# Two more of ten probability copies on ScalarE, placed between its exponentials, and high parts of the attention output on GpSimd

## The reference

```
x = x + attn(layernorm(x))          # 16 heads of 16; q and k layer-normed per head; causal softmax
x = x + ffn(layernorm(x))
  ffn:  h = h + attention(rmsnorm(h))      # 16 heads of 64, latent kv of rank 32, rope on 32, causal softmax
        h = h + moe(rmsnorm(h))            # one shared expert, 8 routed experts of 128, the best 2 chosen
attention:  att = softmax(mask(q k^T));  y = att v;  y @ Wo
```

## Time and profile before

| | us |
|---|---|
| median of 3 runs (3696.23 to 3699.96) | 3697.05 |
| the profiled execution's own time | 3699.16 |
| span of its profile, first to last instruction | 3697.5 |

### The profile page before, as it was taken

How to read it: one execution, slowest core, us unless ns; L and a number is a source line. 1 busy time by engine, 2 the same in 40 slices (tenths; PEclk the granted TensorE clock), 3 DMA queues, 4 the chain that set the end, 5 groups by cost and what they waited for, 6 DMA issues and landing times.

```text
span 3697.5 us, 82731 instructions
## 1 busy us (share of the span) xinstructions
PE 3354.6 (91%) x31744; PEld 2632.8 (71%) x31744; DVE 2763.8 (75%) x5950; ACT 2406.8 (65%) x6426; POOL 1085.9 (29%) x778
## 2 busy tenths in 40 slices
PE   2599999999999999999999999999999999999998
PEld 2477677776767777677776767777677776767776
DVE  3676877878777776877778777777877778777775
ACT  1666667666676766667666676766667666676764
POOL 0424222242412424222242412424222242412420
PEclk9799999999999999999999999999999999999999
DMA  3000000000000000000000000000000000000000
GB/s 80 1 7 1 13 2 7 7 7 7 1 13 2 7 7 1 13 1 7 7 7 7 1 13 2 7 7 1 13 2 7 7 7 7 2 13 2 7 2 7
DMA packets 33766, 28.95 MB, mean 8 GB/s; under 512 B 8864, under 2 KB 33312, under 8 KB 33376
## 3 DMA queue, kind: packets, MB, share of 16 engines
q1 hardware_dynamic: 33376, 23.68, 2.2%
HBM read 15.28 MB, written 8.39 MB: 6 GB/s over the span
## 4 chain that ended last, share of the span: by engine, by line
PE 71%; ACT 14%; DVE 10%; issue 3%; POOL 1%; SPq 1%; DMA 0%; ACTq 0%; POOLq 0%; DVEq 0%
PE bank L670 14%; PE scores L782 11%; PE bank L681 8%; ACT prob L953 6%; PE scores L657 5%; PE bank L806 5%; PE scores L733 4%; PE scores L658 4%; PE scores L756 3%; PE bank L617 3%; PE bank L641 3%; PE scores L659 3%; DVE negmax L1192 2%; ACT qkt L898 2%; PE scores L653 1%
## 5 line engine op out<-in xcount | busy, mean ns | idle before, releaser
L953 ACT ACTIVATE prob<-scores,negmax 128x128 f32<-128x128 f32 (+3 forms) x2048 | 1057.8, 535 | 186.3 <-DVE negmax L1192 180.6
L1192 DVE TENSOR_REDUCE negmax<-scores 128x1 f32<-128x128 f32 (+3 forms) x2048 | 872.6, 481 | 56.9 <-PE scores L659 42.4
L670 PE MATMUL bank<-ident,prob 128*128 128x128 f32 x5120 | 725.6, 279 | 50.6 <-DVE probt L1200 43.6
L1200 DVE COPY probt<-bank 128x512 f32<-128x512 f32 x896 | 596.1, 683 | 171.0 <-PE bank L670 165.3
L670 PEld LDWEIGHTS bank<-ident,prob 128*128 128x128 f32 x5120 | 544.1, 141 | 163.6 <-issue 66.6
L659 PE MATMUL scores<-mask,ident 128*128 128x128 bf16 x2048 | 438.1, 225 | 0.0
L953 ACT ACTIVATION_READ_ACCUMULATOR prob<-scores,negmax 128x1 f32 x2048 | 436.1, 213 | 0.0
L657 PE MATMUL scores<-khh,qt 128*128 128x256 f32 (+2 forms) x1024 | 416.3, 407 | 13.3 <-POOL kll L545 13.3
L486 POOL TENSOR_TENSOR otl<-onm,oth 128x512 fp32r<-128x512 f32 x96 | 122.6, 1277 | 888.8 <-ACT oth L898 888.8
L497 POOL TENSOR_TENSOR rq<-ssq,expo 128x32 f32<-128x32 f32 x64 | 359.9, 5632 | 39.6 <-DVE ssq L1163 39.6
L481 POOL COPY rexp<-rsum 128x512 f32<-128x512 f32 x128 | 78.0, 610 | 981.8 <-DVE rsum L1204 981.8
(11 more groups left out here) (187 smaller groups left out, 6654.6 us busy)
## 6 DMA issues: line engine op xcount, KB each, us to landing
x_in<-in_x_rows SPq DMA_DIRECT2D x16, 512.0 KB, 3.8
out_rows<-x SPq DMA_DIRECT2D x16, 512.0 KB, 2.9
r_gu<-in_wg SPq DMA_DIRECT2D x2, 512.0 KB, 5.0
r_gu<-in_wu SPq DMA_DIRECT2D x2, 512.0 KB, 5.7
r_d<-in_wd SPq DMA_DIRECT2D x1, 1024.0 KB, 7.1
r_wqt<-in_wq_nope_t SPq DMA_DIRECT2D x1, 512.0 KB, 6.7
r_wqr<-in_wq SPq DMA_DIRECT2D x2, 256.0 KB, 8.3
r_wob<-in_wo SPq DMA_DIRECT2D x1, 512.0 KB, 5.3
```

The source lines that it names most:

```text
L670: ins = nc.tensor.transpose(bank[4 + n % 2][:, q * P:(q + 1) * P], prob[:, u % 2, q, i * P:(i + 1) * P], ident[:, :])
L953: nc.scalar.activation(prob[:, u % 2, q, 0:n], bank[q][:, 0:n], ACT.Exp, bias=negmax[:, a, u, q:q + 1], accum_out=sums[:, a, u, q:q + 1]). ...
L1192: nc.vector.tensor_reduce(negmax[:, a, u, M * part:M * part + M], scores[:, M * part:M * part + M, 0:n], axis=AX.X, op=ALU.max, negate=Tru ...
L1200: nc.vector.tensor_copy(probt[:, u % 2, i], bank[4 + n % 2][:, :]).then_inc(probt_dve.sem, 1)
```

## The change

ScalarE's blocks become 0, 2, 4, 7 and 9 of ten, and each is copied behind a given exponential of the next unit: `COPY_AFTER` maps a block to the `part` behind which it stands. VectorE keeps blocks 1, 3, 5, 6 and 8. So on ScalarE the copy of block 0 stands between the second and third exponential of t1 (ahead of the output copy), that of block 2 between the third and fourth exponential of t2, that of block 4 between the third and fourth of t3, and those of blocks 7 and 9 behind all four of the next t0. For all groups but the last of an attention, GpSimd makes the high part from `onm` itself, just ahead of its subtraction, and ScalarE does not. The high part of the last group stays on ScalarE.

```
-ACT_COPIES = tuple(n in (2, 5, 8) for n in range(NT * (NT + 1) // 2))
+COPY_AFTER = {0: 1, 2: 2, 4: 2, 7: 3, 9: 3}
+
+def copy_after(n):
+    return COPY_AFTER.get(n % (NT * (NT + 1) // 2))

 def acts(n):
-    return ACT_COPIES[n % len(ACT_COPIES)]
+    return copy_after(n) is not None
...
 # GpSimd, spread_sums
+                pool.wait_ge(onm_ready.sem, onm_ready.at(b, a * NG + g + 1))
+                nc.gpsimd.tensor_copy(oth[:, g], onm[:, :]).then_inc(oth_ready.sem, 1)
                 pool.wait_ge(oth_ready.sem, oth_ready.at(b, a * NG + g + 1))
...
 # ScalarE, attend
-                if u < UNITS and here:
-                    for part in range(NM // 2):
-                        exps(b, a, u, part)
-                if u % NT == 1 and u > NT:
-                    copy_out(b, a, u // NT - 1)
-                if 0 < u <= UNITS:
-                    mine = [i for i in range(tile_of(u - 1) + 1) if acts(first_block(u - 1) + i)]
-                if u < UNITS and here:
-                    for part in range(NM // 2, NM):
-                        exps(b, a, u, part)
-                for i in mine:
-                    copy_block(b, a, u - 1, i)
-                if u % NT == 2 and u > NT:
-                    split_out(b, a, u // NT - 1)
+                if u > 0:
+                    mine = [i for i in range(tile_of(u - 1) + 1) if acts(first_block(u - 1) + i)]
+                for part in range(NM):
+                    if u < UNITS and here:
+                        exps(b, a, u, part)
+                    for i in mine:
+                        if copy_after(first_block(u - 1) + i) == part:
+                            copy_block(b, a, u - 1, i)
+                    if part == NM // 2 - 1 and u % NT == 1 and u > NT:
+                        copy_out(b, a, u // NT - 1)
```

## The result

The changed kernel takes 3747.55 us (median of 4 runs, 3746.21 to 3748.88); the kernel before, timed beside it, 3697.97 (4 runs, 3696.23 to 3699.96). The ratio of the changed to the kernel before is 1.0134, 95% interval 1.0116 to 1.0151: slower by 49.6 us, where 46.9 were forecast. The profiled span grew from 3697.5 to 3744.8 us, by 47.3.

The account below looks back on a forecast made before the run. TensorE's own work bounds the second attention, a loop through three engines the first. Per sequence 1.60 us (first attention) + 1.33 (second), times 16 = 46.9, on 3697.05 gives 3744 us; own range 3725 to 3762.

Parts of the forecast that it names:

- K: New chain: block 4's transposes, ScalarE copy, t3's fourth exponential, next t0's fourth score; at least 2.04 us.
- Steady groups of the second attention, 0.12: Next t0's fourth score comes 2.04 us behind the transposes of block 4 instead of 1.92: 0.12 us per group.
- First group of the second attention, 0.56: Copy of block 0 delays t1's third exponential, 0.44 us, plus 0.12 from block 4's copy: 0.56 us.
- Last group of the second attention, 0.53: Transposes of blocks 6, 7 come 2.04 us behind those of 4, 5, instead of 1.51: 0.53 us.
- Steady groups of the first attention, 0.23: t3's fourth exponential starts at 1517.29 instead of 1517.06, behind block 4's copy: 0.23 us late per group, nothing given back.
- step (4): First attention, steady group: t0's fourth score 0.23 us late; VectorE's block 5 copy precedes t0's maxima, first exponential some 0.3 later.
- step (3): First attention, steady group: without the high-part copy ScalarE idles for block 4; t3's fourth exponential 0.23 us late, gain eaten.
- First group of the first attention, 0.91: Copies of blocks 0, 2 and 4 bring t0's fourth score at 1714.74 instead of 1713.83: 0.91 us; no removed high-part copy helps.
- A: Rival: relieved VectorE pulls the first attention's loop along, t1's maxima 0.4 us earlier; faster, 3678 us; chance 11%.
- B: Rival: the busier of VectorE and ScalarE paces the first attention, falling by 0.03; no change, 3695 us; chance 7%.
- C: Rival: each ScalarE copy ahead of an exponential takes 0.61 us instead of 0.48; slower still, 3773 us; chance 11%.
- D: Rival: only the first groups pay, for copy of block 0, 0.48 and 0.44 us; 3712 us; chance 9%.

Follow-up runs that it names:

- the four-block kernel: Kernel before, with high parts on GpSimd and ScalarE copying blocks 2, 5, 9 behind the exponentials, 7 between t0's third and fourth: 3686.86 us, ratio 0.9966.
- the three-block one: Kernel before (ScalarE copies blocks 2, 5, 8 behind the exponentials), with only the high parts moved to GpSimd: 3686.36 us, ratio 0.9966.

## Why the prediction was right

- **What bounds each attention.** Held. The second attention's steady group is still full of TensorE's work (15.20 of 15.20), the first's is a loop through three engines, and taking 256 copies from VectorE brought it nothing.
- **K = 0.69 + 0.48 + 0.87 = 2.04.** Measured 0.69 + 0.50 + 0.82 = 2.01. The last term was read where three exponentials of 512 stand ahead of the fourth without a copy between; behind a copy it is 0.82. The run with block 4 one exponential earlier shows K as a chain: it grew by one exponential.
- **Steady groups of the second attention, 0.12.** Measured 0.09, as K is 2.01. I had written it as a wait that the score's row would show; the row shows none (1604.59 in the first group), and only its distance from the transposes, 2.01 in place of 1.92, tells of it.
- **First group of the second attention, 0.56.** Measured 0.53; the 0.44 for the copy of block 0 goes with the experiment that removed it (48.93 to 48.48, 0.45). The step that I estimated at 0.61 is 0.63 (1596.15 to 1596.78).
- **Last group of the second attention, 0.53.** Measured 0.40. K took 2.01, which adds 0.50 to the 1.51 of before, and TensorE reaches the output projection with all of it. Inside the projection 0.11 is taken back: from its first weight load to the first add it is 4.72 us before (1632.59 to 1637.31) and 4.61 in the changed kernel (1654.56 to 1659.17), at a granted clock of 1.00 in both. Why is open.
- **Steady groups of the first attention, 0.23.** Measured 0.24, by the steps: t3's fourth score waits 0.94 (0.9), block 5 waits 0.29 (0.3), t0's fourth score 0.48 (0.5). That the steps add 0.49 and the high parts give 0.26 back was one net number in the prediction; the runs separate them (12.89, 13.15, 13.64, 13.39). What the prediction did not say is that K does not bind alone there. Its step (4) has VectorE's copy of block 5 ahead of t0's maxima, as a delay in step with K; that chain is as long as K's (4.05 us with K and without it), and keeps the group at 13.40 when K is gone. The step and its size were right; that K is the one new wait was not, in this attention.
- **Last group of the first attention, 0.23.** Measured 0.06 to 0.18. I had carried the steady group's number over without working it out. From `onm` to `onm` the group is 0.17 longer (12.44 to 12.61); in some sequences 0.11 comes back behind it.
- **First group of the first attention, 0.91.** Measured 0.99 in the usual sequence. K brings t0's fourth score 0.90 late, as forecast. The other 0.09 comes behind it: from t0's fourth score to t1's first it is 2.84 us (1736.48 to 1739.32), and 2.75 before. Here the second chain, 4.05 us from block 5's transposes at 1735.27, ends later than K.
- **High parts on GpSimd.** 0.614 us each against a bound of 0.61, and no engine waits for it. "Worth 0 on the path by itself" was right only in the sense it was meant, that the gain comes through step (3): done alone it is worth 13 us.
- **The sum.** The stages give 2.6 x 16 = 42 where I had 46.9. The missing term is the clock: 5.1 us by the four long groups, and 0.35 by the one of 17.05. That the total is so near the forecast is luck in part: the two errors nearly cancel.
- **Rivals.** A and B need a gain from the relieved VectorE; none of the ten runs shows one, and the four-block kernel is as fast as the three-block one, no faster. The Trainium skill's advice to offload work to ScalarE when VectorE is saturated (page "Perfetto Trace Analysis", section "Optimizing Scalar/DVE Operations") did not apply: VectorE was idle for 1.5 of 13.15 us, and with fewer copies it only waited longer for TensorE than before. C needs 0.61 between copy and exponential; it is 0.48 to 0.50. D, only the first groups, falls with 0.24 in the steady ones.

## What to carry to other kernels

In a loop of several engines, price a move of work by its place in the receiving engine's order, not by the load: a copy that must wait for TensorE delays everything that stands behind it, and here one exponential earlier cost some 88 us more at equal load, and one later some 7 less. A removed wait is worth only what the next one leaves (0.20 and 0.30 for banks came in where 0.48 for an exponential went). Test the parts of a compound change one by one: here one half alone gained 13 us and the other alone lost 62.

## What the runs showed of the hardware

A few short waits of TensorE were enough to lower its clock. In the changed kernel the gaps ahead of t2's scores are 0.64, 0.34, 0.83 and 0.33 us, and the granted clock still fell from 1.00 (2.4 GHz) to 0.50 (1.2 GHz) in 4 of 15 sequences (12 of 15 with block 4 behind), which made the group 1.2 to 1.4 us longer than the 16.70 of the others. With 0.34 in place of 0.83 it fell in none of six kernels. Two matmuls whose result nobody reads, which leave 0.61 of the 0.83, kept it at 1.00 in all 15 sequences of two kernels. The Trainium skill, page "TensorE: Matmul & The Clock Gate", section "A second HAM failure mode: psum-queue depth-cycling", says that frequent small idle times between groups of matmuls can make the clock swing between its levels; these rows agree with it. Why it falls in some sequences and not in others that begin alike is open.
